# Attention by whole batches instead of by half batches, with every second exponential read from PSUM

## The reference, cut to what matters

```
q = (query @ Wq.T + bq).reshape(n, s, H, d).transpose(0, 2, 1, 3)
k = (key @ Wk.T + bk).reshape(n, t, H, d).transpose(0, 2, 1, 3)
v = (value @ Wv.T + bv).reshape(n, t, H, d).transpose(0, 2, 1, 3)
att = jnp.einsum('bhsd,bhtd->bhst', q, k) / jnp.sqrt(jnp.float32(d))
att = jnp.where(pad_mask == 0, jnp.float32(-1000000000.0), att)
att = jnp.where(subsq_mask == 0, jnp.float32(-1000000000.0), att)
prob = jax.nn.softmax(att, axis=-1)
out = jnp.einsum('bhst,bhtd->bhsd', prob, v)
```

## Time and profile before

| | before |
|---|---|
| median of 3 runs (lowest, highest) | 694.4 us (692.1, 694.56) |
| the profiled execution, by the device's time | 694.07 us |
| its span, first to last instruction | 692.2 us |
| PE, DVE, ACT, POOL busy | 93%, 68%, 44%, 51% of the span |
| mean granted TensorE clock | 0.957 |
| first scores of pair 1 / 6 / 7 | 45.94 / 179.88 / 213.87 us |
| first routed slot | 296.31 us |

### The profile page before, as it was taken

How to read it: one execution, slowest core, us unless ns; L and a number is a source line. 1 busy time by engine, 2 the same in 40 slices (tenths; PEclk the granted TensorE clock), 3 DMA queues, 4 the chain that set the end, 5 groups by cost and what they waited for, 6 DMA issues and landing times.

```text
span 692.2 us, 14875 instructions
## 1 busy us (share of the span) xinstructions
PE 640.6 (93%) x4418; PEld 537.2 (78%) x4419; DVE 468.6 (68%) x1037; ACT 305.4 (44%) x677; POOL 349.8 (51%) x403
## 2 busy tenths in 40 slices
PE   8899999999978879679999999999999999999695
PEld 7787887887856669567888788878887888889595
DVE  7688677688754946666667667766766766774467
ACT  5465556556543343423444444444443444443232
POOL 3881011011054763877789389479886683003553
PEclk9899999999997888889999999999999999999799
DMA  8827524516921043342654344444465231101433
GB/s 280 305 104 263 213 87 156 212 39 251 349 77 62 16 152 107 129 145 77 213 178 172 122 160 171 139 157 148 165 212 174 83 121 38 38 16 50 119 97 117
DMA packets 47910, 98.95 MB, mean 143 GB/s; under 512 B 4736, under 2 KB 23808, under 8 KB 47872
## 3 DMA queue, kind: packets, MB, share of 16 engines
q1 hardware_dynamic: 36192, 50.40, 20.6%
q0 software_dynamic: 10976, 47.72, 20.4%
q10 hardware_dynamic: 704, 0.33, 0.2%
HBM read 57.15 MB, written 39.19 MB: 139 GB/s over the span
## 4 chain that ended last, share of the span: by engine, by line
PE 71%; DVE 13%; issue 5%; ACT 4%; another core or an unknown queue 3%; POOL 1%; DVEq 1%; DMA 1%; ACTq 0%; SPq 0%; POOLq 0%
PE ps_s L788 25%; PE ps_o L821 9%; PE ps_o L822 4%; PE ps_t L584 4%; PE ps_o L596 3%; PE ps_s L572 3%; PE ps_s L750 3%; PE ps_t L798 3%; PE ps_t L511 2%; DVE nmax L1311 2%; PE ps_s L567 1%; PE ps_x L511 1%; PE ps_s L798 1%; PE ps_x L809 1%
## 5 line engine op out<-in xcount | busy, mean ns | idle before, releaser
L788 PE MATMUL ps_s<-ring,xTh 128*128 x516 | 153.0, 418 | 0.0
L1787 POOL TENSOR_TENSOR ring<-stage,ring 128x512 fp32r<-128x512 f32 x80 | 100.6, 1291 | 1.2
L788 PEld LDWEIGHTS ps_s<-ring,xTh 128*128 128x128 f32 x516 | 89.2, 191 | 14.8 <-issue 0.3
L821 PE MATMUL ps_o<-ring,hTh 128*128 x258 | 96.7, 412 | 3.5 <-DVE hTl L1615 3.5
L1606 DVE TENSOR_TENSOR ag<-ps_s,up_bias 128x512 f32<-128x512 f32 x129 | 89.0, 690 | 13.1 <-PE ps_s L788 10.4
L1775 POOL TENSOR_TENSOR ve<-mv,eps 128x2 f32<-128x2 f32 x16 | 4.0, 250 | 161.8 <-DVE mv L1343 148.3
L788 PE MATMUL ps_s<-ring,xTl 128*128 x258 | 80.5, 393 | 0.0
L982 ACT ACTIVATE probT<-ps_t 128x512 f32<-128x512 f32 x64 | 38.3, 598 | 80.4 <-PE ps_t L584 74.0
L822 PE MATMUL ps_o<-ring,hTl 128*128 x258 | 72.6, 281 | 0.0
L1969 POOL DMA_INDIRECT gath<-rows_out,idx_out x32 | 31.9, 998 | 76.3 <-DMA rows_out<-y_row 56.6
L1094 ACT ACTIVATE ps_s<-ag 128x256 f32<-128x256 f32 x129 | 50.2, 389 | 40.6 <-DVE ag L1606 39.2
(11 more groups left out here) (274 smaller groups left out, 1464.1 us busy)
## 6 DMA issues: line engine op xcount, KB each, us to landing
rows_in<-y_row SPq DMA_DIRECT2D x8, 3328.0 KB, 12.2
stage<-in_w POOLq DMA_DIRECT2D x12, 1536.0 KB
stage<-in_w POOLq DMA_DIRECT2D x12, 768.0 KB, 5.3
up_bias<-in_bias POOLq DMA_DIRECT2D x12, 768.0 KB, 4.5
xrow<-rows_in SPq DMA_DIRECT2D x43, 128.0 KB, 2.2
rows_out<-y_row SPq DMA_DIRECT2D x43, 128.0 KB, 1.7
cbuf<-in_ctx SPq DMA_DIRECT2D x8, 256.0 KB, 3.1
xn_all<-xn2p SPq DMA_DIRECT2D x8, 256.0 KB
```

The lines of the kernel that those rows point to most:

```text
L788: last = pe_.matmul(ps_s[:, i, :], x[:, c, :], weights(place, off + c * 2 * HR + i * 2 * D, 2 * D), start=n == 0, stop=n == 5)
L821: pe_.matmul(ps_o[:, :], hTh[i][:, c, :], weights(place, a, 2 * D), start=i == 0 and c == 0, stop=False)
L1787: last = pool.tensor_tensor(lo_ap[:, c:c + PIECE], src[:, c:c + PIECE], hi_ap[:, c:c + PIECE].bitcast(f32), ALU.subtract)
```

## The change

A batch is no longer cut in two units. `scores` takes all four row groups of a batch in turn, after four mask matmuls, and `values` all four column groups. Half of a batch's heads (banks 0 and 1 of `ps_s`) go the old way: maximum, subtraction, `exp_first` of 128x1024. For the other half (banks 2 and 3) DVE takes the maxima only (`softmax_bias`), scales them, and `exp_second` on ACT reads the scores from PSUM in eight instructions of 128x128, each with its column of maxima as the bias. The scores of the next batch wait for both (`shifted` and two of `exp_done` a batch). `probT` holds a whole batch, and its place is new. The order of steps on all engines, the spins of pair 7 (four in place of one, at each filler) and the places of the scatters are new.

```
@@ order of the steps
-            return ["r", "n", "l"]
+            return ["n", "r", "l"]
...
-        todo = ["k0"] + (["n"] if batch_in(p) is not None else []) + ["k1", "q0", "q1", "r", "v", "l"]
-        return todo + ([] if isinstance(p, int) and p == PAIRS - 2 else AHEAD)
+        todo = ["k0", "k1", "q0"] + (["n"] if batch_in(p) is not None else []) + ["q1", "v"]
+        return todo + (["r", "l"] if isinstance(p, int) and p == PAIRS - 2 else ["cT", "r", "xT", "l"])
@@ PE
+            def scores(p, par, b):
+
+                if not (isinstance(p, int) and p == 0 and b == 0):
+                    pe.wait_ge(shifted, p * 2 + b)
+                    pe.wait_ge(exp_done, (p * 2 + b) * 2)
+                for j in range(4):
                     pe_.matmul(ps_s[:, j, :].rearrange("p (g t) -> p g t", g=4), ident_b[:, :],
                                mask_b[:, bass.ds(p * 2 + b, 1), :].broadcast_to([P, 4, P]), start=True, stop=False)
                 for g in range(4):
                     for k in (k_hi, k_lo):
-                        for j in (2 * u, 2 * u + 1):
+                        for j in range(4):
...
+            def prob_transposes(batch, j):
+
+                pe.wait_ge(exp_done, batch * 2 + j // 2 + 1)
+                if not (isinstance(batch, int) and batch == 0 and j == 0):
+                    pe.wait_ge(pt_copied, batch * 4 + j)
...
+            def values(b, par, batch):
+
+                pe.wait_ge(pt_copied, batch * 4 + 4)
...
                 for g in range(4):
+                    for j in range(4):
+                        last = pe_.matmul(ps_o[32 * j:32 * j + VW, g * P:(g + 1) * P], v_sb[par][:, b, 4 * g + j, :],
+                                          probT[:, j, g, :], start=True, stop=True)
...
-            SPIN = 1
+            SPIN = 4
...
+                def filler():
+
+                    if last:
+                        pe.wait_ge(xb_free, base_of(p, first))
+                        spin(SPIN, ps_x[:, 0:D])
@@ ACT
+            def exp_second(batch, jj):
+
+                if jj == 0:
+                    sc.wait_ge(bias_of_max, batch + 1)
+                    if not (isinstance(batch, int) and batch == 0):
+                        sc.wait_ge(pt_ready, 4 * batch)
+                for g in range(4):
+                    last = act.activation(prob[1][:, jj, g, :], ps_s[:, 2 + jj, g * P:(g + 1) * P], ACT.Exp,
+                                          bias=nbias[:, jj, g:g + 1], scale=1.0 / HD ** 0.5)
+                if jj == 1:
+                    last.then_inc(exp_done, 1)
...
+                    prev = p * 2 - 1
+                    prob_copy(prev, 0)
+                    prob_copy(prev, 1)
                     put("k0")
+                    prob_copy(prev, 2)
+                    prob_copy(prev, 3)
+                    put("k1")
+                    out_copy(prev)
+                    exp_first(p * 2)
+                    exp_second(p * 2, 0)
+                    put("q0")
+                    exp_second(p * 2, 1)
@@ DVE
+            def softmax_bias(batch):
+
+                ve.wait_ge(scores_ready, batch + 1)
+                vec.tensor_reduce(nmax1[:, :, :], ps_s[:, 2:4, :].rearrange("p j (g t) -> p j g t", g=4), AX.X, ALU.max,
+                                  negate=True).then_inc(max1_done, 1)
+                ve.wait_ge(max1_done, batch + 1)
+                vec.tensor_scalar(nbias[:, :, :], nmax1[:, :, :], 1.0 / HD ** 0.5, None, ALU.mult).then_inc(bias_of_max, 1)
@@ POOL
+            def paced_scatters(tiles, step):
+
+                for i, t in enumerate(tiles):
+                    gp.wait_ge(pt_ready, step + i + 1)
+                    scatter(t)
```

More of the change, by code:

```diff
@@ new lines, in pair @@
+                if first:
+                    pe.wait_ge(xb_free, len(FIRST) - 1)
+                else:
+                    ahead = 2 if isinstance(p, int) and p == PAIRS - 1 else 4
+                    pe.wait_ge(xb_free, base_of(p, first) - ahead)
+                    pe.wait_ge(masks_ready, 2)
+                    pe.wait_ge(router_in, 32)
+                scores(p, par, 0)
+                if first:
+                    put("cT")
+                    put("xT")
+                    put("k0")
+                    put("k1")
+                    put("q0")
+                else:
+                    prev = p * 2 - 1
+                    prob_transposes(prev, 0)
+                    put("k0", (0,))
+                    filler()
+                    prob_transposes(prev, 1)
+                    put("k0", (1,))
+                    filler()
+                    prob_transposes(prev, 2)
+                    put("k1", (0,))
+                    filler()
+                    prob_transposes(prev, 3)
+                    put("k1", (1,))
+                    filler()
+                    values(1, 1 - par, prev)
+                    put("q0", (0,))
+                    filler()
+                    out_transposes(prev)
+                    put("q0", (1,))
+                    if not last:
+                        put("n")
@@ new lines, in pair @@
+                scores(p, par, 1)
+                prev = p * 2
+                prob_transposes(prev, 0)
+                put("q1", (0,))
+                filler()
+                prob_transposes(prev, 1)
+                put("q1", (1,))
+                filler()
+                prob_transposes(prev, 2)
+                put("v", (0,))
+                filler()
+                prob_transposes(prev, 3)
+                put("v", (1,))
+                filler()
+                values(0, par, prev)
@@ L717, in _ @@
+                if tail:
+                    put("cT", again=first)
+                if last:
+                    put("n")
+                put("r")
+                out_transposes(prev)
+                if tail:
+                    put("xT", again=first)
+                put("l")
             each_pair(pe, pair)
@@ L1442, in pair @@
                     ln1_stats(2)
+                softmax_bias(p * 2)
                 put("k0")
+                put("k1")
+                if not first:
+                    if further:
+                        ln1_stats(p + 2)
+                    norm(p - 1, 1)
+                    residual(p - 1, 1)
+                put("q0")
                 if not last:
                     put("n")
-                if not first:
-                    norm(p - 1, 1)
                 if isinstance(p, int) and p == PAIRS - 3:
                     choose(0, 0)
+                if last:
+                    choose(0, 1)
+                    choose(1, 1)
+                softmax_shift(p * 2 + 1)
+                if not first:
+                    ln2_apply(p - 1)
                 if isinstance(p, int) and p == PAIRS - 2:
@@ L1452, in pair @@
                     row_numbers(0)
[L1453 to L1467 removed]
+                softmax_bias(p * 2 + 1)
+                put("q1")
+                if further:
+                    put("cT", first)
+                    ln1_apply(p + 2)
                 if last:
@@ L1470, in pair @@
                 norm(p, 0)
+                if further:
+                    put("xT", first)
+                residual(p, 0)
+                put("l")
                 if last:
@@ L1933, in _ @@
             load_raw2(1)
+            gp.wait_ge(xn2_saved, 16 * 6)
+            gp.wait_ge(rows_ready, 2)
+            for t in range(8, 12):
+                scatter(t)
             gp.wait_ge(normed, B)
```

245 lines of the change are left out of this document (67 added, 178 removed).

## The result

The change makes the kernel slower: 731.39 us median (727.2 to 732.69) against 694.48 us (692.1 to 698.3), a ratio of 1.052, 95% interval 1.045 to 1.058. The forecast was 705 us in a range of 686 to 727: the direction held, and the time lies above the range. The profiled execution took 731.27 us, with a span of 729.4, 37.2 more than before.

The account below looks back on a forecast made before the run. TensorE's own list was taken to bound pairs 1 to 5; the change closes a longer round with clock falls. Pairs 1 to 5 +14.1, pair 0 -1, pair 6 -4, end +2: +11 on 694.07, so 705 us, range 686 to 727.

Parts of the forecast that it names:

- The packing: Scores and values on four groups: a set of four costs 0.11 us like two, TensorE's list 22.6 us a pair, from 26.8.
- the round: Each half of a pair closes a loop of scores, transposes, values and exponentials: 13.4 us, 26.9 a pair; TensorE waits 4.3.
- pair 6: The 4.82 us wait comes from twelve scatters in a row, of which three tiles remain: 30.0 us for 33.99, -4.
- the estimate for four row tiles: By the skill's 3.07 times for four row tiles, a set of four takes 0.03 us more; not in the sum.
- The clock: After TensorE's waits, one half-clock stretch of 3.4 us per half costs 1.3 us: 26.9 + 2.7 = 29.6 us a pair.
- Pair 0: The first pair has two sets of scores instead of four, but the same round once: -1 us, bounds -3 and +2.
- The end: Pair 7 and the last batch, with longer fillers and halves of 15.4 us: +2 us, bounds -4 and +8.
- The rival "the clock stays up": The loop closes but TensorE's clock does not fall in pairs 1 to 5: 688 us (683 to 697), chance 0.17.

Follow-up runs that it names:

- spins_placed: The changed kernel plus five matmuls of zeros at each of a pair's two waits, ahead of the second half's masks and the normed rows' transposes: 703.5 us, ratio 1.019.
- spins_placed_two: spins_placed with two matmuls of zeros in place of four at each filler of pair 7 and in the last batch: 705.8 us, ratio 1.015.
- tuned_spin2: shift_both with VectorE and ScalarE reordered, and two zero matmuls for four at pair 7's and the last batch's fillers: 664.8 us, 0.991 of the kernel before (671.5 there).
- shift_both: The changed kernel with the second half of the heads done as the first, VectorE subtracting and one large exponential replacing eight small: 711.5 us, ratio 1.026.

## Why the prediction was wrong

Two terms of its sum failed: the clock's 2.7 us a pair, which the runs show as 3.8, and "+2" for pair 7 and the last batch, measured at +17.4. The packing, the round and pair 6 held.

- *The packing* was right: sets at 0.11 and not the 0.14 of the estimate for four row tiles, values at 1.01, masks at 0.95 us, and PE is busy for 22.0 to 22.3 us in a pair at full clock, for 22.6.
- *The round* was right. The half is 13.35 us for 13.4, its wait 2.64 for 2.6. With the clock held up by spins a pair is 27.15 for 26.9. One detail was off: the second half's wait is a single one of 2.2 us, not 1.5 in two pieces, since r's copy stands behind small exponentials.
- *The clock* failed, in its size. "I count one for each half" at 1.3 us gave 2.7 a pair; the runs show 3.8. The price of the low clock was right: 1.3 us in 3.4 is 0.39 for each, and 0.41 was measured. What was too small is how long it lasts: ten stretches of 3.4 us are 34 us, and pairs 1 to 5 spend 48.8 at half clock, read in windows of 0.5 us. There are fewer falls than forecast: behind each of the five waits of 2.6 us, but behind two of the five of 2.2. Yet five of these seven stretches last 6.8 us, and pair 1 begins in one that started before it. That is 5.6 of the 8.3 us that pairs 1 to 5 exceed the forecast; the rest is the round, 1.3, and pair 1, which in spins_placed too took 1.2 longer than the three behind it.
- *Pair 0* came out at +1.8 for -1, inside its bounds.
- *Pair 6* is 4.1 us shorter for 4. The wait of 4.82 us there was put down to the scatters, and it moved with them: most of them are issued in pair 7 now, and there the output copy starts 2.2 us behind its values, in spins_placed_two 5.9.
- *The end* is the largest miss: "+2 (bounds -4 and +8)" measured +17.4. Its halves were summed at full clock, 15.4 us each, and the first is 20.6:

```profile
237.43 1.11 PE L589 MATMUL ps_t<-const,prob 128*128 128x128 f32 x4
238.33 2.53 PE L616 MATMUL ps_x<-y_row 128*128 128x256 f32 x8
...
247.29 1.08 PE L599 MATMUL ps_o<-probT,v_sb 128*32 128x128 f32 x32
...
254.28 1.87 PE L572 MATMUL ps_s<-mask_b,ident_b 128*128 128x512 bf16 x4 [2.44 <-ACT prob L1009]
```

```profile
250.54 0.60 ACT L995 ACTIVATE outT<-ps_o 128x512 f32<-128x512 f32 x1 [4.27 <-remote]
251.03 1.05 ACT L999 ACTIVATE prob<-prob 128x1024 f32<-128x1024 f32 x1
```

  From the masks at 233.72 on, masks and scores take 3.7 us for 2.0, at half clock; the four steps of transposes 9.9 for 8.6, with a first filler of 2.4 for 1.7; values to the large exponential 3.7 for 1.6, by the late output copy; the exponentials 3.25 for 3.15. So what the forecast charged in pairs 1 to 5 it left out where the clock was at 0.80 already. The last values start 48.1 us behind the first masks for the forecast's 38, and the stretch behind them is 3.5 us longer where it was to be 2 shorter; TensorE's wait for the last normed rows there is 4.15 us for 2.19. With spins in the pairs' waits 6.1 of the 17.4 went; the fillers are up to 7, by tuned_spin2; the remaining 4 to 5 us, the last batch's four transposes in a row, say, were not taken apart by a run.
- *The rival "the clock stays up"* rested on the Trainium skill, "TensorE: Matmul & The Clock Gate", section "Why this matters for your kernels": only idle gaps above a length that none of these waits reaches are to be avoided between bursts. Seven of ten waits of 2.2 to 2.6 us were followed by a fall, and filling them gave 19 us back. The trace doesn't bear the rule out for gaps that come every 13 to 17 us. Nor is a long wait the only thing that stands ahead of a fall: in the kernel before the clock stood at half again from 215.6 to 219.2 us, and in the 7 us ahead of that TensorE waited once, 0.28 us.

The sum of the misses: pair 0 +2.8, pairs 1 to 5 +8.3, end +15.4, which is the 26 us between 705 and 731.

## What to carry to other kernels

When an edit takes work off the busiest engine, lay out the round that its waits close before counting the gain: here 4.2 us of TensorE's list a pair went and the pair grew by 4.5, and the same packing gave 3.1 a pair once what the next scores wait for was taken out of ScalarE's queue of copies. Price a wait of TensorE twice, as idle time and as what the lower clock costs behind it, in every stage that it reaches, and fill a wait that can't be removed, at the very instruction that waits: with five of a pair's ten spins at the wrong place they gave nothing, with all ten at the right ones 28 us. And where an engine is at 99%, look for the next bound before promising what a shorter list brings.

## What the runs showed of the hardware beyond that

In the eleven traces taken where the kernel before ran at 691 to 696 us, instructions that wait for matmuls start late during a burst of scatters. Where nothing else holds it the output copy starts 0.07 to 0.15 us behind the modelled end of its values, and here up to 5.9 us, mostly within a microsecond of the end of a scatter's transfer, as above. The kernel before shows it as well: behind the wait of 4.82 us stand a copy and a row maximum that start 4.9 and 5.4 us behind the matmuls they wait for. In the four traces taken where that kernel ran at 671 us the same scatters come, and the copy starts at most 1.1 us behind. One chip gave both levels at different times. The kernel of shift_both_tuned was profiled at both, with spans of 681.9 and 667.9 us: 3.4 of the 14 us lie ahead of the first routed slot and 10.6 behind it, where indirect gathers run at the end and ScalarE's late starts stand in the one trace and not in the other. That these stalls are the 14 to 20 us between the two levels is argued from their sum, not shown: what holds TensorE's completions back, and why it does so at one time and not at another, stays open.
